# A recommender's pooled history: each group of four scaled rows summed by one 512-column product instead of four 128-column ones

## What is computed

```python
items_emb = item_table[items]                     # 2048 x 128
user_emb = user_table[users]
hist_emb = user_table[history_users]              # 2048 x 100 x 128
scores = jnp.einsum('bhd,bd->bh', hist_emb, user_emb)
user_his_emb = jnp.einsum('bh,bhd->bd', scores, hist_emb)
x = jnp.concatenate([items_emb, user_his_emb, user_emb], axis=1)
x = _dice(_batchnorm(x @ W1 + b1, g1, be1), a1)   # 384 -> 1024
x = _dice(_batchnorm(x @ W2 + b2, g2, be2), a2)   # 1024 -> 512
return x @ W3 + b3                                # 512 -> 1
```

## Time and profile before

| | |
|---|---|
| time, median of three runs | 1003.19 us |
| time of the profiled execution | 1003.54 us |
| its span, first to last instruction | 1001.5 us |
| tiles, from the first group's scaling to the last | 46 to 828 us |
| mean granted TensorE clock | 0.743 of 2.4 GHz |
| PE, weight loads, DVE, ACT, POOL busy | 655, 612, 521, 339, 491 us |
| gathers of rows, each | 432 in the groups' loops, 953 ns |

### The profile page before, as it was taken

How to read it: one execution, slowest core, us unless ns; L and a number is a source line. 1 busy time by engine, 2 the same in 40 slices (tenths; PEclk the granted TensorE clock), 3 DMA queues, 4 the chain that set the end, 5 groups by cost and what they waited for, 6 DMA issues and landing times.

```text
span 1001.5 us, 16389 instructions
## 1 busy us (share of the span) xinstructions
PE 655.3 (65%) x3743; PEld 611.8 (61%) x3743; DVE 520.6 (52%) x1339; ACT 338.9 (34%) x879; POOL 490.8 (49%) x580
## 2 busy tenths in 40 slices
PE   4464655647474747466567465756766469999998
PEld 3463655547473736456467455755665469888888
DVE  7553444344453526354436354644344526999748
ACT  3111222223132313132223132332223237778546
POOL 6646544454555454636454635545544534281025
PEclk8776675757675666766676677858676679999999
DMA  7112111111111111111111111111111110000000
GB/s 218 38 35 44 35 34 35 35 42 33 42 36 39 30 45 26 44 27 42 32 38 33 45 25 42 35 34 39 40 34 33 43 22 1 2 0 1 1 1 2
DMA packets 17236, 34.61 MB, mean 35 GB/s; under 512 B 8104, under 2 KB 8400, under 8 KB 17168
## 3 DMA queue, kind: packets, MB, share of 16 engines
q0 software_dynamic: 14208, 29.13, 11.8%
q1 hardware_dynamic: 2960, 4.67, 1.4%
HBM read 33.76 MB, written 0.01 MB: 34 GB/s over the span
## 4 chain that ended last, share of the span: by engine, by line
PE 44%; another core or an unknown queue 26%; issue 15%; ACT 6%; DVE 4%; ACTq 4%; DVEq 1%; PEld 0%; PEldq 0%
PE ps L1489 14%; PE ps L1549 10%; PE ps L1409 7%; ACT scaled L1244 4%; PE ps L1425 3%; ACTq L1244 2%; PE ps L1475 2%; PE ps L1499 1%; PE ps L1564 1%; PE ps L1388 1%; ACT h L1230 1%; PE ps L1633 1%; PE ps L1430 1%; ACTq L1265 1%
## 5 line engine op out<-in xcount | busy, mean ns | idle before, releaser
L520 POOL DMA_INDIRECT rows<-in_L_rec_user_table_dram,slot_idx x432 | 411.6, 953 | 378.9 <-ACT scaled L1244 252.3
L1489 PE MATMUL ps<-ident,scaled 128*128 128x128 f32 x982 | 211.5, 384 | 228.1 <-ACT scaled L1244 188.0
L1489 PEld LDWEIGHTS ps<-ident,scaled 128*128 128x128 f32 x982 | 188.8, 285 | 245.6 <-issue 237.1
L1244 ACT ACTIVATE scaled<-rows,work 128x128 f32 (+1 forms) x491 | 157.3, 392 | 256.6 <-remote 162.0
L834 DVE TENSOR_TENSOR prod<-rows,ps 128x512 f32<-128x512 f32 x122 | 83.7, 686 | 152.9 <-issue 79.4
L711 DVE SCALAR_TENSOR_TENSOR h<-ps,col_no 128x1024 f32<-128x1024 f32 (+1 forms) x34 | 39.2, 1161 | 164.4 <-ACT ranked L1211 75.6
L1549 PE MATMUL ps<-h,w 128*128 128x256 f32 (+1 forms) x576 | 113.3, 356 | 1.0 <-DVE h L1064 1.0
L1409 PEld LDWEIGHTS ps<-wide,h 128*128 128x128 f32 x512 | 100.3, 297 | 16.9 <-issue 16.9
L1409 PE MATMUL ps<-wide,h 128*128 128x104 f32 x512 | 102.5, 382 | 9.7 <-issue 9.7
L1549 PEld LDWEIGHTS ps<-h,w 128*128 128x128 f32 x576 | 99.6, 190 | 12.8 <-issue 1.2
L840 DVE TENSOR_REDUCE work<-prod 128x512 f32 (+1 forms) x122 | 83.7, 686 | 35.3 <-issue 20.4
(11 more groups left out here) (219 smaller groups left out, 806.4 us busy)
## 6 DMA issues: line engine op xcount, KB each, us to landing
rows<-in_L_rec_user_table_dram,slot_idx POOLq DMA_INDIRECT x432
w<-in_L_rec_W_dram SPq DMA_DIRECT2D x1, 2048.0 KB
w<-in_L_rec_W_dram SPq DMA_DIRECT2D x1, 1536.0 KB
h<-in_r_history_users_dram SPq DMA_DIRECT2D x2, 400.0 KB, 3.5
wide<-in_L_rec_user_table_dram,own_idx POOLq DMA_INDIRECT x5
wide<-in_L_rec_item_table_dram,own_idx POOLq DMA_INDIRECT x5
last_row<-in_L_rec_user_table_dram SPq DMA_DIRECT2D x1, 64.0 KB
last_item<-in_L_rec_item_table_dram SPq DMA_DIRECT2D x1, 64.0 KB
```

The costliest lines, as they stand in the source:

```text
L520: nc.gpsimd.indirect_dma_start(rows[:, s, :], None, user_table, bass.IndirectOffsetOnAxis(slot_idx[:, s:s + 1], 0)).then_inc(landed[s], 16)
L1244: nc.scalar.activation(scaled[:, j, :], rows[:, bass.ds((g & (GROUPS - 1)) * GROUP + j, 1), :], ACT.Copy, scale=score[:, bass.ds(g * GROUP ...
L1489: mm = nc.tensor.matmul(pooled_ps, scaled[:, j, :], ident[:, :], start=False, stop=False, skip_group_check=True)
```

## The change

`scaled` becomes three buffers. In tiles 0 to 14 a group's four scaled rows are one moving operand of 512 columns against the identity as stationary operand: `quarter_ps`, all of PSUM bank 1, collects by user what slots 0, 1, 2, 3 of the groups give, in four quarters. At the tile's end ACT copies the 512 columns to `quarters`, and in the next tile four products, ahead of the two transposes, turn and add the quarters into a third block of `turn_ps`, which `both_T` takes along (384 columns in place of 256). `layer1_pooled` reads it there. The last tile adds row by row as before. PE waits once a group, for all four rows (`rows_free`). The last row's product comes after group g0. The first four groups of a tile alternate between two buffers, so ACT waits for a sum two groups back or not at all; the loop uses buffer 0 and waits for the group before; the last group has buffer 2. `pooled` is given by the last product itself. `hold` loses the increment, so that a wait stands at the instruction that follows; two waits of POOL and two of DVE keep it (`hold_apart`). Addresses and columns in `scale_rows` are held in registers taken once a group.

```diff
-        scaled = sb("scaled", [P, GROUP, D])
+        scaled = [sb(f"scaled{i}", [P, GROUP, D]) for i in range(3)]
+        quarters = sb("quarters", [P, GROUP, D])
...
-        both_T = sb("both_T", [P, 2 * P])
+        both_T = sb("both_T", [P, 3 * P])
...
+        quarter_ps = ps[:, 1, :].rearrange("p (q d) -> p q d", d=D)
...
-        turn_ps = ps[:, 5, 0:2 * P]
+        turn_ps = ps[:, 5, 0:3 * P]
...
         def hold(eng, semaphore, value):
+            if not isinstance(value, int) or value > 0:
+                eng.wait_ge(semaphore, value)
+
+        def hold_apart(eng, semaphore, value):
+            hold(eng, semaphore, value)
             if not isinstance(value, int):
-                eng.wait_ge(semaphore, value)
                 eng.sem_inc(passed, 1)
-            elif value > 0:
-                eng.wait_ge(semaphore, value)
...
-                    hold(pool, rows_free, GROUPS * r + (q - GROUPS + 1))
+                    hold_apart(pool, rows_free, GROUPS * r + (q - GROUPS + 1))
...
-                hold(dve, keys_cut, before)
+                hold_apart(dve, keys_cut, before)
...
-                hold(dve, sorted_out, before + 1)
+                hold_apart(dve, sorted_out, before + 1)
...
                     nc.scalar.activation(h1[:, m, t * P:(t + 1) * P], l1_ps[:, m, :], ACT.Identity,
                                          bias=b1c[:, m:m + 1]).then_inc(l1_kept, 1)
 
-            def scale_rows(g, t, after):
-                by_slot = t == TILES - 1 and after is end_scaled
-                count = GROUP - 1 if by_slot else GROUP
-                if not by_slot:
+            rows_flat = rows.rearrange("p s d -> p (s d)")
+
+            def scale_rows(g, t, buf, behind):
+                if not isinstance(g, int):
+                    g = act.snap(g).with_bounds(max_val=HIST * (t + 1) // GROUP - 1)
+                hold(act, scored, g + (t + 1))
+                if behind is not None:
+
+                    hold(act, pair_summed, g + (2 - behind))
+                at = (g & (GROUPS - 1)) * (GROUP * D)
+                pair = g * GROUP + t * GROUP
+                if not isinstance(g, int):
+                    at, pair = act.snap(at), act.snap(pair)
+                for j in range(GROUP):
+                    sc = nc.scalar.activation(scaled[buf][:, j, :], rows_flat[:, bass.ds(at + j * D, D)], ACT.Copy,
+                                              scale=score[:, bass.ds(pair + j, 1)])
+                sc.then_inc(rows_free, 1)
+
+            def scale_end(g, t):
+
+                last = t == TILES - 1
+                g = act.snap(g).with_bounds(max_val=HIST * (t + 1) // GROUP - 1)
+                if not last:
                     hold(act, scored, g + (t + 1))
-                for j in range(count):
-                    if by_slot:
+                at, pair = act.snap((g & (GROUPS - 1)) * (GROUP * D)), act.snap(g * GROUP + t * GROUP)
+                for j in range(sum(n for _, n in END_PARTS) if last else GROUP):
+                    if last:
                         act.wait_ge(end_scored, END_PARTS.index(max(part for part in END_PARTS if part[0] <= j)) + 1)
-                    if j == 0:
-
-                        hold(act, pair_summed, g + (t + 1))
-                    nc.scalar.activation(scaled[:, j, :], rows[:, bass.ds((g & (GROUPS - 1)) * GROUP + j, 1), :], ACT.Copy,
-                                         scale=score[:, bass.ds(g * GROUP + (t * GROUP + j), 1)]).then_inc(
-                                             slot_scaled if j < GROUP - 1 else after, 1)
+                    sc = nc.scalar.activation(scaled[2][:, j, :], rows_flat[:, bass.ds(at + j * D, D)], ACT.Copy,
+                                              scale=score[:, bass.ds(pair + j, 1)])
+                    if last or j == GROUP - 1:
+                        sc.then_inc(slot_scaled if last else end_scaled, 1)
...
-                for i in range(3):
-                    scale_rows(g0 + i, t, rows_free)
+                for i in range(GROUPS):
+                    scale_rows(g0 + i, t, i % 2, 0 if i == 0 else None if i == 1 else 1)
                     if i == 0:
                         act.wait_ge(turned, t + 1)
-                        nc.scalar.activation(both_T[:, :], turn_ps, ACT.Copy).then_inc(both_kept, 1)
-                    elif t:
+                        n = 3 * P if t else 2 * P
+                        nc.scalar.activation(both_T[:, 0:n], turn_ps[:, 0:n], ACT.Copy).then_inc(both_kept, 1)
+                    elif t and i < 3:
                         keep_layer1(t - 1, 4 * i - 4)
                     elif i == 1:
                         keep_rows(1)
-                with act.Fori(g0 + 3, g1) as g:
-                    scale_rows(g, t, rows_free)
+                with act.Fori(g0 + GROUPS, g1) as g:
+                    scale_rows(g, t, 0, 0)
                 if t + 2 < TILES:
                     keep_rows(t + 2)
-                scale_rows(g1, t, end_scaled)
+                scale_end(g1, t)
                 if t == 0:
                     act.wait_ge(par_ready, 2)
                 act.wait_ge(pooled, t + 1)
-                nc.scalar.activation(pooled_T[:, :], pooled_ps, ACT.Copy).then_inc(pooled_kept, 1)
+                if t < TILES - 1:
+                    nc.scalar.activation(quarters[:, :, :], quarter_ps, ACT.Copy).then_inc(pooled_kept, 1)
+                else:
+                    nc.scalar.activation(pooled_T[:, :], pooled_ps, ACT.Copy).then_inc(pooled_kept, 1)
...
-            pe.sem_inc(pair_summed, 1)
+            pe.sem_inc(pair_summed, 2)
...
             def layer1_pooled(t):
-                pe.wait_ge(pooled_kept, t + 1)
+                if t == TILES - 1:
+                    pe.wait_ge(pooled_kept, t + 1)
+                else:
+                    pe.wait_ge(both_kept, t + 2)
                 for m in range(M1):
-                    mm = nc.tensor.matmul(l1_ps[:, m, :], w1[:, 1, m * P:(m + 1) * P], pooled_T[:, :],
+                    mm = nc.tensor.matmul(l1_ps[:, m, :], w1[:, 1, m * P:(m + 1) * P],
+                                          pooled_T[:, :] if t == TILES - 1 else both_T[:, 2 * P:3 * P],
                                           start=False, stop=True, skip_group_check=True)
                     if m % 4 == 3:
                         mm.then_inc(l1_done, 1)
 
-            def add_rows(g, t, end):
-
-                for j in range(GROUP - 1 if end and t == TILES - 1 else GROUP):
-                    if j < GROUP - 1:
-                        hold(pe, slot_scaled, g * (GROUP - 1) + (t * (GROUP - 1) + j + 1))
-                    elif end:
-                        pe.wait_ge(end_scaled, t + 1)
-                    else:
-                        hold(pe, rows_free, g + 1)
-                    mm = nc.tensor.matmul(pooled_ps, scaled[:, j, :], ident[:, :], start=False, stop=False,
+            def add_rows(g, t, buf, first=False):
+
+                hold(pe, rows_free, g + 1)
+                if t == TILES - 1:
+                    for j in range(GROUP):
+                        mm = nc.tensor.matmul(pooled_ps, scaled[buf][:, j, :], ident[:, :], start=(first and j == 0), stop=False,
+                                              skip_group_check=True)
+                else:
+                    mm = nc.tensor.matmul(quarter_ps, ident[:, :], scaled[buf][:, :, :], start=first, stop=False,
                                           skip_group_check=True)
                 mm.then_inc(pair_summed, 1)
+
+            def add_end(t):
+
+                if t == TILES - 1:
+                    for j in range(sum(n for _, n in END_PARTS)):
+                        pe.wait_ge(slot_scaled, j + 1)
+                        mm = nc.tensor.matmul(pooled_ps, scaled[2][:, j, :], ident[:, :], start=False, stop=False,
+                                              skip_group_check=True)
+                else:
+                    pe.wait_ge(end_scaled, t + 1)
+                    mm = nc.tensor.matmul(quarter_ps, ident[:, :], scaled[2][:, :, :], start=False, stop=False,
+                                          skip_group_check=True)
+                mm.then_inc(pooled, 1)
 
             for t in range(TILES):
                 begin.append(end_of(pe, t))
                 g0, g1 = begin[t] >> 2 if t else 0, begin[t + 1] >> 2
-                pe.wait_ge(last_ready, t + 1)
                 if t:
                     pe.wait_ge(pooled_kept, t)
-                nc.tensor.matmul(pooled_ps, last_scaled[:, :], ident[:, :], start=True, stop=False,
-                                 skip_group_check=True)
-                add_rows(g0, t, False)
+                add_rows(g0, t, 0, True)
+                pe.wait_ge(last_ready, t + 1)
+                if t == TILES - 1:
+                    nc.tensor.matmul(pooled_ps, last_scaled[:, :], ident[:, :], start=False, stop=False, skip_group_check=True)
+                else:
```

(20 more changed lines are left out.)

## The result

The changed kernel takes **978.57 us** (median of 5 runs, 976.32 to 981.55) against 1003.19 (1000.81 to 1003.52): ratio 0.9759, 95% interval 0.9732 to 0.9786. The prediction said 1034 us and slower; 978.6 lies at the lower end of its range, near rival B.

What follows compares the result with a forecast made beforehand. No engine was full; a ring of waits among ACT, GpSimd, DVE and PE bounded the kernel. 1003.5 + 10.5 + 25.5 - 6 = 1033.5, said as 1034 us; range 975 to 1080, the forecast's own 1020 to 1050.

Steps and rivals of the forecast that it cites:

- rival B: PE's results: fewer PE instructions, not order, would make them punctual and shorten ACT's waits; 972 us, chance 0.18.
- Step 1: Last group of a tile, 15 seams: 3.52 us against 2.72 before, +0.7 each, +10.5 us in all.
- Step 2: Second group of a tile, 15 tiles: transposes 3.02 us later, a new gather hole of 1.7 us each, +25.5 us.
- PE's late results: PE to ACT: results held back once gathers run about 4 us, until about 2.9 us after the last one.
- rival A: Tile start: later transposes fall into the hold on PE's results, hole 4.3 us instead of 1.7; 1073 us, chance 0.29.
- Step 3: Groups of the loop: ACT restarts every 3.8 us instead of 2.96, covered by 5.0 us of gathers; cost 0.
- Step 4: Waits folded into the next instruction and fewer register steps: 0.4 us a tile saved, -6 us.
- Rival C: PE's product is cheap, by a faster clock or as the skill page has it; 998 us, chance 0.07.
- Rival D: Whole kernel: the change does nothing, both sides hidden or folded waits costing what they did; 1003 us, chance 0.09.
- remote idle on ACT under 300 us in all: ACT's waits the profile calls remote: a total below 300 us was named as a sign the prediction was wrong.

Runs made afterwards that it cites:

- before_by_tile: Kernel before, with seven dummy products ahead of the transposes in six tiles and PE's single wait per group in six (two overlap); 1000.56 us against 999.18, single runs.

## Why the prediction was wrong, by its steps

*Step 1, right in the price of a seam.* From the end group's first scaling to the copy of the quarters the median is 3.44 us, against 3.52 worked out (3.42 less PE's queue) and 2.72 before; three seams took 2.49 to 2.70, less than before, as the pair of products found the clock at 1.00 (at 657.19 it takes 1.12 us). Over the 15 seams it is 48.6 us against 45.7, +2.9 for the +10.5 of the sum: 3.9 us come back at the last one, which took 7.83 before. A pair of 512-column halves takes 1.92 us at clock 0.50 and 1.02 at 1.00 (303.45 and 286.45 in the timeline): by columns, not by instructions. The 0.52 us for such a pair that the prediction estimated from the Trainium skill ("TensorE: Matmul & The Clock Gate", section "Back-to-back issue gap") isn't seen in these records.

*Step 2, its parts right and its sum wrong: this is the step that failed.* *both_T* is copied 6.00 us after the tile's first scaling (3.05 + 3.02 = 6.07 forecast), and there is a hole: 1.27 us in the median, 0.84 to 1.64, of which 0.30 follows any gather, where 1.7 was said. "A hole of 1.7 us where there was none: 15 x 1.7 = +25.5 us" added it to a tile whose other pauses were taken as fixed. They weren't: each pause of the gathers is when PE's late results come out, so a pause put early replaces part of the later ones. Measured in before_by_tile, the same delay is worth -1.6 us a tile (-3.1 to -0.4 in four tiles), not +1.7. That it is worth as much in the other tiles, tile 14 above all, isn't shown. The text had both halves of this at hand, the hold until about 2.9 us after the last gather and the hole, and used the first only to make the second worse (rival A).

*Step 3, right in size* for the low clock: scalings in the loop are 3.70 us apart (90.70, 94.40, 98.10, granted clock 0.50), 3.8 forecast, and four gathers take 5.0.

*Step 4.* -6 us said; -3 us for ACT and PE on a late chip, nothing for DVE, and +0.7% on a punctual one, which no bound below nothing had allowed for.

*Rival A* came about in one tile of 15: in the changed kernel *both_T* comes some 6.4 us into the tile, without a hole of 4 us, in all but the last (9.64, hole 4.79). Past 8 us, in before_by_tile, three tiles went 3.0 and 0.1 us up and 1.8 down, so its price stays open. *Rival B* came nearest in time (972), by luck: four products give back 1.6 of 6 us at most, and its signs don't hold, as sums and keys are still waited for (262.8 and 139.9 us). *Rival C* falls: most seams ran at the low clock, and the time is 19 us below its 998. *Rival D* falls on the late chip; on punctual ones it is what the later transposes do (0.9998).

The condition named in the prediction, "remote idle on ACT under 300 us in all", came true (190.0 us, of 407.0 before). It was to mean that the results are no longer late. For layer 1 they aren't; most of the rest changed its name, not its length, since the waits that have PE's name, ahead of the same four kinds of ACT's work, grew from 104.3 to 305.9 us.

## What to carry to other kernels

In a ring of engines, where each waits for the next, a new pause is not added to the old ones until it is asked what comes out in it: redo the order of the whole round from the pause on. If a result is held back for as long as some other engine is busy, where its pauses fall matters more than how many there are. And a gain read on one chip may be a loss on another: the waits that made this change pay were absent on four of the six chips of these sets, so measure on several before keeping it.

## What was unexpected of the hardware

The same program, 748 or 1003 us by chip. On the late ones, small instructions slow down while gathers run, not PE's sums alone. Three of four dependent DVE instructions in the changed kernel, late chip:

```profile
50.88 0.17 DVE L820 TENSOR_SCALAR over<-rest 128x2 f32<-128x2 f32 x1 [0.73 <-DVE rest L817]
52.31 0.16 DVE L822 TENSOR_TENSOR rest<-rest,over 128x2 f32<-128x2 f32 x1 [1.26 <-DVE over L820]
53.74 0.17 DVE L824 RECIPROCAL over<-rest 128x2 f32<-128x2 f32 x1 [1.27 <-DVE rest L822]
```

and on a punctual one:

```profile
46.48 0.17 DVE L820 TENSOR_SCALAR over<-rest 128x2 f32<-128x2 f32 x1
46.68 0.16 DVE L822 TENSOR_TENSOR rest<-rest,over 128x2 f32<-128x2 f32 x1
46.87 0.17 DVE L824 RECIPROCAL over<-rest 128x2 f32<-128x2 f32 x1
```

1.43 us from one to the next against 0.20. PE's layer 1 products crawl in the same way inside the run of twelve gathers:

```profile
298.11 0.37 PE L1495 MATMUL ps<-both_T,w 128*128 128x128 f32 x1 [1.85 <-issue]
...
300.24 0.37 PE L1495 MATMUL ps<-both_T,w 128*128 128x128 f32 x1 [1.76 <-issue]
...
302.37 0.37 PE L1495 MATMUL ps<-both_T,w 128*128 128x128 f32 x1 [1.76 <-issue]
```

2.13 us each, where sixteen take 3.03 us once the gathers have stopped (305.15). 1.43 and 2.13 are two and three times 0.71. So what the prediction called PE's late results looks, though no run tests it, like engines that get through few instructions beside the gathers. What is slow in those chips, and why not in the others, stays open; no kernel here could take it away.
